# Gate and up projections of the last feed-forward layer as seven block products in place of eight, tokens in two halves of 1024

## What is computed

```python
gate = jnp.einsum('bsh,ih->bsi', x, gate_w) * gate_scale     # 1376 rows of weights, 512 columns
up = jnp.einsum('bsh,ih->bsi', x, up_w) * up_scale
inter = jax.nn.silu(gate) * up
out = jnp.einsum('bsi,hi->bsh', inter, down_w) * down_scale
```

## Time and profile before

| | |
|---|---|
| median of 3 runs | 1731.55 us (1725.85 to 1733.9) |
| profiled execution, its own time | 1734.02 us |
| its span, first to last instruction | 1732.2 us |
| mean granted TensorE clock | 0.987 |
| PE busy | 1670.9 us, 96%, 8354 matmuls |
| DVE, ACT, POOL busy | 1029.2, 876.6, 577.1 us (59, 51, 33%) |
| chain that ended last, PE lines 1906 and 1917 | 14% and 7% of the span |

### The profile page before, as it was taken

How to read it: one execution, slowest core, us unless ns; L and a number is a source line. 1 busy time by engine, 2 the same in 40 slices (tenths; PEclk the granted TensorE clock), 3 DMA queues, 4 the chain that set the end, 5 groups by cost and what they waited for, 6 DMA issues and landing times. The chain is left out here.

```text
span 1732.2 us, 26128 instructions
## 1 busy us (share of the span) xinstructions
PE 1670.9 (96%) x8354; PEld 1395.9 (81%) x8354; DVE 1029.2 (59%) x2915; ACT 876.6 (51%) x2303; POOL 577.1 (33%) x893
## 2 busy tenths in 40 slices
PE   5888999999999999999999999999999899999999
PEld 4667897788888888888888888888887788888887
DVE  7866425667767767767767767767767453223212
ACT  4476435556556556556556556556646332121111
POOL 4611002446346346346346346346345000000000
PEclk9979999999999999999999999999999999999999
DMA  5200455211111111124111111111110231000000
GB/s 161 71 1 1 181 197 206 73 38 49 61 37 50 62 38 50 61 86 170 62 37 50 61 38 50 61 37 49 62 37 19 86 96 39 1 25 1 25 0 25
DMA packets 57056, 106.24 MB, mean 61 GB/s; under 512 B 5408, under 2 KB 23840, under 8 KB 52832
## 3 DMA queue, kind: packets, MB, share of 16 engines
q1 hardware_dynamic: 56032, 104.09, 18.2%
q10 hardware_dynamic: 896, 0.56, 0.2%
HBM read 76.32 MB, written 28.31 MB: 60 GB/s over the span
## 5 line engine op out<-in xcount | busy, mean ns | idle before, releaser
L1633 PE MATMUL ps_q<-kv_w_hi,o_hi 128*128 128x512 f32 x512 | 206.6, 404 | 4.4 <-DVE o_lo L138 2.9
L1633 PE MATMUL ps_q<-kv_w_lo,o_hi 128*128 128x512 f32 x512 | 201.8, 394 | 0.0
L1633 PE MATMUL ps_q<-kv_w_hi,o_lo 128*128 128x512 f32 x512 | 201.6, 394 | 0.0
L138 POOL TENSOR_TENSOR kv_w_lo<-w_raw,kv_w_hi 128x512 fp32r<-128x512 f32 x128 | 163.8, 1297 | 75.9 <-ACT kv_w_hi L133 75.9
L1575 PE MATMUL ps_q<-h_hi,kv_w_hi 128*128 128x512 f32 x448 | 182.3, 407 | 2.6 <-PEq L933 1.4
L1575 PE MATMUL ps_q<-h_hi,kv_w_lo 128*128 128x512 f32 x448 | 175.2, 391 | 0.0
L1575 PE MATMUL ps_q<-h_lo,kv_w_hi 128*128 128x512 f32 x448 | 175.2, 391 | 0.0
L133 ACT ACTIVATE kv_w_hi<-w_raw 128x512 fp32r<-128x512 f32 (+1 forms) x240 | 126.6, 566 | 64.5 <-POOL w_raw L516 62.3
L100 POOL TENSOR_TENSOR factors_ln<-ve_ln,half 128x1 f32<-128x1 f32 (+1 forms) x64 | 39.6, 618 | 335.4 <-DVE ve_ln L96 335.0
L1875 DVE SCALAR_TENSOR_TENSOR f_act<-f_ps_r,f_scale,f_act 128x512 f32<-128x512 f32 x44 | 33.0, 751 | 191.5 <-PE f_ps_r L1906 190.2
L1223 ACT ACTIVATE prob<-prob,neg_max 128x128 f32<-128x128 f32 x256 | 100.2, 392 | 87.5 <-DVE neg_max L1378 87.4
(11 more groups left out here) (217 smaller groups left out, 4560.6 us busy)
## 6 DMA issues: line engine op xcount, KB each, us to landing
w_raw<-in_wq_g SPq DMA_DIRECT2D x16, 1024.0 KB, 4.9
w_raw<-in_wo_g SPq DMA_DIRECT2D x16, 1024.0 KB, 4.7
k_scratch<-kv_stage SPq DMA_DIRECT2D x32, 256.0 KB, 2.5
v_scratch<-kv_stage SPq DMA_DIRECT2D x32, 256.0 KB, 2.1
k_raw<-k_scratch SPq DMA_DIRECT2D x32, 256.0 KB, 3.4
v_raw<-v_scratch SPq DMA_DIRECT2D x32, 256.0 KB, 3.8
x<-in_x SPq DMA_DIRECT2D x16, 256.0 KB, 2.9
out<-x SPq DMA_DIRECT2D x16, 256.0 KB, 2.1
```

The lines of the kernel that those rows point to most:

```text
L138: return dve.tensor_tensor(parts[LO], src, parts[HI].bitcast(F32), ALU.subtract)
L1633: done = pe.matmul(ps_q[:, half, :], o[b][i][:, half, h, :], wo[j][:, h, :], start=(h == 0 and m == 0), stop=(h == GROUP - 1 and m == 2))
```

## The change

Eleven chunks of rows become one single chunk (the last, 2 x 5 chunks being paired) and five pairs, the tokens two halves of 1024 in place of four groups of 512. There are 12 steps: per half one step with the single chunk and five with a pair. In a step with a pair, gate is a two by two block product: 2 blocks of 128 rows by 2 blocks of 256 inner columns of the weights (A), and 2 inner blocks by 2 blocks of 512 tokens (B). Seven products of 6 matmuls (`CHAIN`) take the place of eight; up likewise.

- `FeedWeights` replaces resident weights: in each step, so twice per pair, 512 KB of gate and of up (256 KB for a single) is loaded, ACT makes seven hi parts of 128x256, POOL four sums of blocks (S1 to S4) and seven lo parts of 128x256, for each of gate and up. There is one set of slots for each, so a hi part of step k+1 is only written once PE has done the last product (P3) of step k. Down weights are loaded per step as well, split by ACT and POOL.
- `FeedTokens` replaces `FeedStart`: for each half, eight tiles are flipped as before (area "B"), and POOL makes differences and sums of them (`sums`, 16 instructions of 256 columns per half, each waiting for the one before), which are flipped too (area "T"): 16 flips per half. POOL, not DVE, applies the layer norm's factors.
- The attention's last unit flips eight tiles in place of four, and the order of its start changes: output of the unit before comes ahead of the first flips. The layer norm's statistics of half 0 are spread, one tile a unit, over the eight units 22 to 29.
- In the attention's block, POOL ends with the lo parts of the single gate and up chunks and the 16 sums of half 0. The first up chunk is loaded and split there too.
- Evacuation: per step with a pair, DVE adds seven products up for gate and seven for up, multiplies four pieces from SBUF with SBUF, and makes four lo parts; ACT copies P1 twice, makes four silu and four hi parts.
- Operand loads in the attention's middle share semaphores by group (`OPERAND_LOADS`).

```diff
+    def sums(self, pool, half, j):
+        first, second = self.tiles[j], self.tiles[4 + j]
+        n = 4 * (4 * half + j)
+        pool.wait_ge(self.t_done, self.flips(half, 0, 2 * j + 1))
+        pool.tensor_tensor(first[:, 0:2 * P], second[:, 0:2 * P], first[:, 0:2 * P], ALU.subtract).then_inc(self.made, 1)
+        pool.wait_ge(self.made, n + 1)
+        pool.tensor_tensor(second[:, 0:2 * P], second[:, 2 * P:4 * P], second[:, 0:2 * P], ALU.subtract).then_inc(self.made, 1)
...
+    def build(self, pool, k):
+        n = self.sums_before(k)
+        self.lo(pool, "A22", k)
+        pool.wait_ge(self.lo_done, self.count(k, "A22"))
+        pool.tensor_tensor(self.block("S1"), self.block("A21"), self.block("A22"), ALU.add).then_inc(self.made, 1)
+        self.lo(pool, "A11", k)
+        pool.tensor_tensor(self.block("S3"), self.block("A11"), self.block("A21"), ALU.subtract).then_inc(self.made, 1)
...
+        for name in FEED_MADE:
+            self.lo(pool, name, k)
...
@@ attention, POOL, after the last unit @@
+                gate.single_lo(pool, 0, gate_raw)
+                up.single_lo(pool, 0, up_raw)
+                for j in range(4):
+                    feed.sums(pool, 0, j)
...
@@ attention, PE, last_pair @@
                     scores(u, 0)
                     output(u - 1, 1, 0)
                     scores(u, 1)
-                    feed_flip(0)
+                    output(u - 1, 1, 1)
                     flip(u, 0, 0)
                     flip(u, 0, 1)
-                    output(u - 1, 1, 1)
+                    turn(0)
+                    turn(1)
                     flip(u, 0, 2)
-                    feed_flip(1)
+                    turn(2)
+                    turn(3)
                     values(u, 0, 0)
-                    feed_flip(2)
+                    turn(4)
                     values(u, 0, 1)
-                    feed_flip(3)
+                    turn(5)
+                    turn(6)
+                    turn(7)
                     second_half(u)
...
@@ feed_forward, POOL @@
+                for k in range(STEPS):
+                    if k == WIDE:
+                        for j in range(4):
+                            feed.sums(pool, 1, j)
+                    if k:
+                        build(up, k)
+                    if k + 1 < STEPS:
+                        build(gate, k + 1)
+                    down_part(k)
+                    if 1 <= k <= 4:
+                        for j in (2 * (k - 1), 2 * (k - 1) + 1):
+                            feed.ln.power(pool, 8 + j)
+                            feed.apply(pool, 1, j)
...
@@ feed_forward, DVE, one step @@
+                    piece_lo(k - 1, last - 2)
+                    total("G", k, "U2")
+                    piece_lo(k - 1, last - 1)
+                    for name in FEED_SUMS[1:]:
+                        total("G", k, name)
+                    for t in range(8):
+                        add(k - 1, t)
...
+                    total("U", k, "U2")
+                    total("U", k, "C11")
+                    multiply_sum(k, "C11")
+                    total("U", k, "U3")
+                    piece_lo(k, 0)
+                    total("U", k, "C21")
+                    multiply_sum(k, "C21")
+                    total("U", k, "C22")
+                    total("U", k, "U4")
+                    piece_lo(k, 1)
+                    multiply_sum(k, "C22")
+                    total("U", k, "C12")
+                    multiply_sum(k, "C12")
...
@@ feed_forward, PE @@
+                for k in range(STEPS):
+                    if k % WIDE == 0:
+                        alone("G", k)
+                        for pos in range(8):
+                            turn(k // WIDE, 1, pos)
+                        alone("U", k)
+                    else:
+                        products("G", k)
+                        multiply_down(k - 1, range(8))
+                        products("U", k)
+                    if k == PAIRED:
+                        for pos in range(4):
+                            turn(1, 0, pos)
+                        multiply_down(k, range(4))
+                        for pos in range(4, 8):
+                            turn(1, 0, pos)
+                        multiply_down(k, range(4, 8))
+                multiply_down(STEPS - 1, range(8))
```

More of the change, by code:

```diff
@@ L169, in build @@
         h3 = split("h3", [P, KC, TOKENS])
[L170 to L182, removed]
@@ L186, in block_sparse_linear @@
+        parts = [sb(f"q_part{i}", [P, 2, 2, P]) for i in range(4)]
+        feed.hold([weights.raw[:, t, :] for t in range(4)] + [part[:, :, :, :].rearrange("p b t n -> p (b t n)") for part in parts])
+        attention(nc, sem, sb, ps, split, x, ident, kv_w, weights, operands, parts, stored, feed, gate, up, wq_g, wo_g, k_scr, v_scr)
+        feed_forward(nc, sem, sb, ps, split, x, kv_w, feed, gate, up, down_c, scales, out)
 def block_sparse_linear(nc, sem, sb, ps, split, x, ident, half, consts, ln, ln_next, x_in, mask_t, w0_t, bias0, load_next, kv_weights, kv_w):
@@ L1793, in _, with build, down_part @@
             def _(pool):
-                def group(g, first, last):
-                    if not last:
-                        for tt in range(4):
-                            ln.power(pool, 4 * (g + 1) + tt)
-                groups(pool, group)
+                def build(w, k):
+                    if k % WIDE:
+                        w.build(pool, k)
+                    else:
+                        w.single_lo(pool, k, w.raw[:, 0, :])
+                def down_part(k):
+                    for m in range(chunks(k)):
+                        pool.wait_ge(down_hi, downs(k, m))
+                        lo_part(pool, down[m], down_raw[:, m, :]).then_inc(down_lo, 1)
@@ new lines, in alone @@
+                def alone(kind, k):
+                    w = weights[kind]
+                    pe.wait_ge(w.lo_done, w.count(k))
+                    for n in range(2):
+                        freed(kind, k, n)
+                        pe.wait_ge(feed.h_lo, feed.flips(k // WIDE, 0, 7))
+                        for c in range(KC):
+                            right = feed.operand((("B11", "B12"), ("B21", "B22"))[c // 2][n])
+                            for m, (a, b) in enumerate(PASSES):
+                                last = pe.matmul(bank(kind, k, n), w.single[a][:, c * P:(c + 1) * P], right[b][:, c % 2, :],
+                                                 start=(c == 0 and m == 0), stop=(c == KC - 1 and m == 2))
+                        last.then_inc(r_done, 1)
@@ new lines, in products @@
+                def products(kind, k):
+                    w = weights[kind]
+                    for name in CHAIN:
+                        left, right = FACTORS[name]
+                        freed(kind, k, name)
+                        pe.wait_ge(w.lo_done, w.count(k, left))
+                        if name == "P6":
+                            pe.wait_ge(feed.h_lo, feed.flips(k // WIDE, 1, 7))
+                        for c in range(2):
+                            stationary = w.left(left, c)
+                            for m, (a, b) in enumerate(PASSES):
+                                last = pe.matmul(bank(kind, k, name), stationary[a], feed.operand(right)[b][:, c, :],
+                                                 start=(c == 0 and m == 0), stop=(c == 1 and m == 2))
+                        last.then_inc(r_done, 1)
```

660 lines of the change are left out of this document (425 added, 235 removed).

## The result

The changed kernel takes **1721.55 us** (median of 7 runs, 1718.92 to 1723.54) against 1731.55 before: 10.0 us less by the medians. The ratio of the two is put at 0.9947 [0.9934, 0.996], which is 6.9 to 11.4 us less. The forecast was 1717.0, 14.6 less. The profiled execution took 1721.22 us, with a span of 1719.4 us, 12.8 shorter than the span before.

What follows compares the result with a forecast made beforehand. The prediction took PE's matmul count to bound the kernel: 120 fewer matmuls (-27.2 us), offset by flips, waits, border, handovers and tail, summed to -14.6 us, from 1731.55 to 1717.0 us, with a range of 1707 to 1731.

Steps and rivals of the forecast that it cites:

- ring waits of T and B flips: Feed-forward flips waiting for banks: +1.8 us for two T phases, +1.3 us for the B flips of half 1.
- Loads of 512 KB are issued some 15 us before use, and 1 MB lands in 4.7: nothing: Weight loads in the feed-forward steps: issued early enough to add no time.
- ACT's hi parts wait for POOL's sums, but nobody waits for ACT then: Steps with a pair: ACT's hi parts (0.41 us each) wait for POOL's sums, delaying no other engine.
- Matmuls: Feed-forward stage: 120 matmuls fewer at 0.2267 us each, -27.2 us.
- 4.8 us for a wider distance: Feed-forward stage: 1464 matmuls at the attention's 0.230 us apart would take 4.8 us longer; kept for the upper end.
- The border: Between attention and feed-forward: PE waits for POOL's lo parts and 16 sums, then runs at lower clock; +2.0 us in all.
- The attention: Attention's last units: statistics spread one tile a unit, -1.5 us; `second_half` starting earlier, -1 us (bounds -2 and +4).
- Handovers: Steps with a pair: a booked allowance of 0.2 us a step, +2.0 us.
- Rival A: DVE and POOL block each other in SBUF: 1 us lost per step, border 3 us longer, 1730 us; chance 0.2.
- 1.7 us of room in the up products: Pair step: DVE's last up sum ends at 11.9 us, PE needs that bank at 13.6.
- Rival B: POOL becomes the bound at 1.30 us a sum: 1788 us, or 1747 in a milder form; chance 0.1 together.
- Rival C: The border does not wait, as sums run faster than 0.5 us or start earlier: 1710 us; chance 0.1.

Runs made afterwards that it cites:

- the two other edits: Changed kernel with POOL's sums of j = 2, 3 of half 0 moved behind the border and half 0's stores one step later: 1712.65 us.
- split sums: Changed kernel with POOL's sums of j = 2, 3 of half 0 moved from the attention's block into the feed-forward block: 1715.02 us.

## Why the prediction was right, and where it was not

The time fell into the range, and the forecast's case held: PE sets the time, the border waits, the rest is small. The measured gain is 4.6 us short of the forecast by the medians. By the profiles (-12.8, of which 1.8 stand already at 345 us, in code that the change doesn't touch) the terms stand so:

| term of the sum | forecast | profile |
|---|---|---|
| 120 matmuls less | -27.2 | -27.2 |
| 12 flips more | +5.2 | +5.3 |
| ring waits of T and B flips | +3.1 | +3.9 |
| handovers in the steps, gate factors behind a single chunk | +3.5 | +2.2 |
| up products of step 7 | 0 | +5.1 |
| tail | +1.3 | +1.1 |
| border: idle time | +5.3 | +3.9 |
| border: lower clock | +1.6 | +2.3 |
| border: wait and slow matmuls of the kernel before | -4.9 | -5.2 |
| attention, and all ahead of it | -2.5 | -4.1, of which 1.8 in unchanged code |
| sum | -14.6 | -12.7 |

**The step that failed** first is "Loads of 512 KB are issued some 15 us before use, and 1 MB lands in 4.7: nothing". I costed the loads by their distance to the use, and did not ask what stands ahead of them in SP's queue. In step 7 these are the eight stores of the first half, and the load went out 5.5 us late. The second step that failed is **"ACT's hi parts wait for POOL's sums, but nobody waits for ACT then"**. This holds in eight of the ten steps. Behind a single chunk the down products are half as long, ACT still stands in front of POOL's sums when P1 is done, and the copy of P1 is behind it. The runs part the two, by the time lost in step 7's up products and right behind them: 5.1 us with the load late and the copy late, 2.4 with the load on time, 3.2 with the copy early, nothing with both put right. By the medians, stores later gave 3.2 us, the early copy alone 3.5 (1.4 of it in and behind step 1, by the lost time), and the early copy on top of the two other edits 5.5 (3.8 by the lost time).

**Matmuls.** The price of 0.2267 was right and the layout did not change it: where nothing is late, the distances of the changed kernel are the same, and 4.8 us for a wider distance weren't needed. The 120 matmuls added back showed each at its full price, with 4.6 us of the 27.2 hidden behind the lateness that the shorter products had uncovered.

**The border** was right in mechanism and in the total (+2.0 forecast, +1.0 by the profile). The sum of 256 columns took 0.74 and not 0.78, with 0.82 behind a wait for itself and 0.70 without, so 16 of them 12.5 us and not 13.8. The lower clock lasted for twelve matmuls and not the seven of the earlier trace rows. Undoing it gave 6.5 us.

**The attention** came out near by two errors that cancel. By the profiles the spread statistics brought 0.9 us (1.8 less 0.9) where 1.5 was forecast, and the last unit 1.7 where 1.0 was. The forecast counted the wait that goes and put the delay by the tiles spread over the units at nothing.

**Handovers** of 0.2 us a step did not exist as such: eight steps lost nothing, and the 1.8 us of step 1 are the 0.4 of P6 for gate's S2 (forecast 0.8) and the late copy. A sum with a flat allowance can come out near for the wrong reason, as it did here.

**Rival A**, contention of DVE and POOL, was real in the rows and cost nothing in time. Groups of DVE's multiplications of up sums in the changed kernel, then POOL's lo parts of up and gate, by form:

```profile
L2127 DVE SCALAR_TENSOR_TENSOR f_product<-f_part_U,f_scale,f_product 128x512 f32<-128x512 f32 x40 | 38.2, 955 | 1.1
L138 POOL TENSOR_TENSOR kv_w_lo<-f_up_raw,kv_w_hi 128x256 fp32r<-128x256 f32 x70 | 55.8, 815 | 44.6 <-ACT kv_w_hi L133 44.6
L138 POOL TENSOR_TENSOR kv_w_lo<-f_gate_raw,kv_w_hi 128x256 fp32r<-128x256 f32 x70 | 50.4, 740 | 20.2 <-ACT kv_w_hi L133 20.2
```

In the view of the tile f_product of the same kernel, DVE's lo parts (min/median/max in ns):

```profile
L138 DVE TENSOR_TENSOR kv_w_lo<-f_product,kv_w_hi x32: 681/693/1658, 1380.7 to 1706.8; 128x512 fp32r<-128x512 f32 x32
```

The multiplications were near 1.0 as the rival said, up from 0.751 in the earlier trace rows (there with one input from PSUM), but PE waited for DVE's sums of products 0.9 us in all (0.7 and 0.2 in the list of waits). The forecast's 1.7 us of room in the up products would explain that, but was not measured by itself. The kernel with early copy and tiny sums settles it for the sums: without their contention it is no faster. For POOL's lo parts it stays open. By the Trainium skill, "SBUF — State Buffer", section "Who interferes with whom", DVE's second read port is shared with GpSimd as an exclusive lock, so the later of two such instructions waits. The single instructions agree (a DVE lo part of up to 1.66 us in place of 0.69, a POOL sum of two columns at 0.71 in place of 0.20), and the mean stays small as most don't meet: half of DVE's lo parts took 0.693 or less.

**Rival B** needed 1.1 us a sum, and it is 0.74. Its mechanism is there nonetheless: 10.7 us more of POOL a step (929.0 us busy in place of 822.2) cost 55 us, and 4.7 us more a step cost 17, nearly all of it in steps 1 and 7. The forecast's 23.4 of 29.9 us described a plain step; the two behind a single chunk have no such room. **Rival C** fell with the drain at 1357.7.

What stays open: where the profiles' differences in unchanged code come from (1.8 us between before and after, and up to 4.9 between two changed kernels, all of it there by 345 us), and what the last unit of the attention is worth by itself; it was not tried.

## What to carry to other kernels

Read each engine's list as a queue: before an instruction is costed at nothing, look at what stands ahead of it in its queue and what that waits for, the queue that issues transfers included. A sum per step hides the odd steps; take the one with the shortest cover (here the one behind a half as long product) by itself. When a saved matmul brings less than its distance, put as many back: what is missing in the difference is lateness that the longer products covered, and may be had by moving one instruction.

## What the runs showed of the hardware

- A POOL sum of two fp32 operands in SBUF took 0.195 us for 2 columns, 0.738 for 256 and 1.29 for 512. The fixed part is 0.19, not the 0.27 that I took from its scalar form in the earlier trace rows.
- A POOL sum of two columns took 0.20 us alone and 0.71 on the mean of ten where it met DVE instructions with two SBUF inputs. A tiny instruction was held up for the length of the other engine's (0.75 us).
- At a block's end whose last work is DVE's add of PE's last product, PE was idle for 1.20 us, before the change and in each kernel with split sums. Matmuls 128x512 at the lower clock behind an idle time: none behind 1.20 us, seven behind 2.50, eight behind 2.99 (and two at nearly full pace ahead of them), seven behind 3.29, fourteen behind 3.65, twelve behind 5.09. The number does not follow the length alone.
- Eight stores of a 128x512 tile, 0.69 us each in SP's queue, hold up every load behind them by 5.5 us.
